# Linear attention in chunks of 64 tokens with a regrouped TensorE slot and a ring of six states

## The chip, the cores and the metric

The kernel runs on one core of a Trainium2 chip. The metric is the device time of one execution in microseconds (us). Three timed runs of the kernel before gave a median of 864.46 us (862.91 to 868.9). A profile was taken of one execution.

## The reference, cut to what matters

One transformer layer over 4 sequences of 2048 tokens of width 256: a causal linear attention with 16 heads of 16, then a mixture of 8 experts of which each token takes two. Around both stand layer norms whose scale, shift and gate come from a small product. The attention is written as a running state:

```
def step(carry, inp):
    S, z = carry
    q_t, k_t, v_t = inp                      # q, k = elu(.) + 1
    S = S + k_t[..., :, None] * v_t[..., None, :]
    z = z + k_t
    num = jnp.einsum('bhde,bhd->bhe', S, q_t)
    den = jnp.maximum(jnp.sum(z * q_t, axis=-1, keepdims=True), EPS)
    return ((S, z), num / den)
...
x = x + ga * attention(layernorm(x) * (1 + ca) + sa)
x = x + gb * moe(layernorm(x) * (1 + cb) + sb)   # top 2 of 8, capacity 1280 rows each
```

## The kernel before, in words

The tokens are 64 tiles of 128, in 16 groups of four. The first phase, up to about 600 us, is attention and routing; the second reads the rows gathered for each expert and adds their results to the output.

The first phase is one list of slots, `run_slots`, which every engine walks with its own `slot_`. Slot n carries the attention of tile n, a quarter of the projections of group n // 4 + 1 (stage 1), a quarter of the second layer norm and row building of group n // 4 - 1, and a quarter of the routing of group n // 4 - 2. The four slots of a group are told apart by q = n % 4. The order within a slot is written out by hand on each engine, and each engine runs it strictly in that order; semaphores hold it until another engine's result is there.

For a tile, the 128 tokens stand against each other in one block. TensorE makes the scores k.q of two heads at a time (`scores`, L1340, 256 columns, 32 rows deep, into the four banks of `SCW`). VectorE multiplies them by the triangle `tri` in two halves of 128x1024 (`masked_scores`, L967). Into the same banks (`OB`) TensorE then adds two things: the queries times the state carried from all earlier tiles (`from_state`, L1360) and the masked scores times the values (`from_tile`, L1376, in two halves of eight heads). Each value row has 17 columns, so that the 17th gives the denominator. The keys are transposed (`key_rows`, L1366), copied by ScalarE to `Kn` (L820) and multiplied by the values to update the state in PSUM (`add_to_state`, L1391, bank `SB`); VectorE copies it to `Sbd` (`state`, L992). The sums leave through ScalarE (`OTs`, L839). One slot later they are transposed to rows (`head_rows`, L1350, bank `MD`), normalised by VectorE (`normalise_heads`, L976 to L983), transposed back (`attention_columns`, L1401, bank `MA`), copied (`ATs`, L824) and multiplied by the output weights (`out_product`, L1409, again bank `MD`). VectorE adds the result to x (`add_out`, L1114).

Stage 1 goes through the banks `PJ[0]` and `PJ[1]`: the transposes of the normalised rows (L1420, slot 0), the four query and key blocks (`stage1_qk`, L1436, two each in slots 1 and 2; ScalarE reads each twice, as EX and as QT or KT, L676 and L677, and VectorE finishes it in `phi`, L1001), and the two value blocks (`stage1_v`, L1446, slot 3). The transposed rows are scaled to `hT_raw` (L658), rounded to a high part (L665) and GpSimd makes the low part (L544). Routing shares the banks: `h2_transposes` (L1468, slot 0), the copies `h2T` (L801), `logits` (L1488), `logit_rows` (L1495, slot 1), `take` (L754), and `positions` (L1555 to L1559, slot 3). GpSimd scatters the rows to the experts' buffers, eight scatters a group (L494), each released by a step of TensorE.

TensorE's order in a slot of the kernel before is: scores; routing rows; first stage 1 block; positions; head rows of tile n - 1; from-state; (stage 1 transposes in slot 0); key rows; first half from-tile; attention columns; second half from-tile; state update; out product of tile n - 1; second stage 1 block; logits in slot 0.

## Time and profile before

| | us |
|---|---|
| median of three timed runs | 864.46 |
| span of the profiled execution | 864.3 |
| TensorE busy in it (PE) | 812.9 |
| VectorE (DVE) | 577.1 |
| ScalarE (ACT) | 488.9 |
| GpSimd (POOL) | 478.9 |

The page gives each engine's busy time and costliest groups of instructions. PE is TensorE's matmuls and PEld its weight loads, which overlap them. L1376 is line 1376 of the kernel. In the timeline a number in brackets is the time that the engine stood idle before the row, and the arrow names what released it.

### The profile page before, as it was taken

To read this page: it belongs to the slowest core of one execution; us is meant where nothing else is said; L and a number is where in the kernel's file an instruction comes from. 1 tells how busy PE (TensorE), PEld (TensorE's weight loads), DVE (VectorE), ACT (ScalarE), POOL (GpSimd) and SP (SyncE) were. 2 spreads that over 40 slices of the span, in tenths; PEclk is the share of its full clock that TensorE was granted. 3 is DMA by queue.
4 is the path that set the end of the run, shared out by engine and by line. 5 is a ranking of instruction groups with operands and counts; after the bars stand their busy time and mean duration, and the time that the engine had idled before them with its cause. 6 is when DMAs were issued, how large, how long until landed. Compare 5 with 4: busy or idle time off the path is not lost.

```text
span 864.3 us, 24637 instructions
## 1 busy us (share of the span) xinstructions
PE 812.9 (94%) x9527; PEld 667.7 (77%) x9527; DVE 577.1 (67%) x1740; ACT 488.9 (57%) x1003; POOL 478.9 (55%) x621
## 2 busy tenths in 40 slices
PE   6899999999999999999999999868999998999994
PEld 4677776777767767777777677558999998999994
DVE  5676676777777867868767767750756655767762
ACT  4665666656757656657657565442655453555551
POOL 2203345664664665646656646564556657666654
PEclk9999999999999999999999999988999999999997
DMA  5589903333332233322222212334476666676653
GB/s 195 186 247 282 284 26 114 85 87 110 67 120 89 76 114 87 86 101 70 72 71 62 64 50 41 62 85 148 82 158 120 151 145 122 152 152 158 121 100 37
DMA packets 71426, 99.02 MB, mean 115 GB/s; under 512 B 7810, under 2 KB 52866, under 8 KB 71320
## 3 DMA queue, kind: packets, MB, share of 16 engines
q1 hardware_dynamic: 38744, 53.93, 23.0%
q0 software_dynamic: 21760, 31.66, 16.2%
q10 hardware_dynamic: 10816, 11.96, 4.5%
q8 instruction: 72, 1.18, 0.6%
q14 instruction: 34, 0.28, 0.1%
HBM read 46.84 MB, written 63.36 MB: 127 GB/s over the span
## 4 chain that ended last, share of the span: by engine, by line
PE 75%; POOL 6%; DMA 6%; DVE 4%; issue 4%; ACT 3%; POOLq 0%; another core or an unknown queue 0%; SPq 0%; DVEq 0%; ACTq 0%
PE PJ L1436 10%; PE SCW L1662 9%; PE MD L1409 7%; PE SCW L1340 7%; PE SCW L1376 7%; PE PJ L1446 5%; PE SCW L1677 4%; PE SCW L1360 4%; PE SCW L1401 4%; DMA out<-EX,desti 3%; PE MD L1350 3%; PE SCW L1366 2%; PE SB L1677 2%; PE MD L1677 2%; POOL hT L544 2%
## 5 line engine op out<-in xcount | busy, mean ns | idle before, releaser
L494 POOL DMA_INDIRECT slot_rows<-Hrow,sloti x128 | 128.0, 1000 | 129.6 <-PE SCW L1366 48.5
L967 DVE TENSOR_TENSOR Sm<-SCW,tri 128x1024 f32<-128x1024 f32 x128 | 150.7, 1219 | 70.9 <-PE SCW L1340 69.0
L612 POOL DMA_INDIRECT out<-EX,desti x80 | 125.3, 1566 | 24.1 <-POOL idle L440 11.4
L1436 PE MATMUL PJ<-hT,w_qkv 128*128 128x512 f32 x384 | 110.1, 419 | 2.4 <-POOL hT L544 1.9
L440 POOL TENSOR_TENSOR idle<-mhalf 128x1 f32<-128x1 f32 x136 | 58.9, 433 | 78.5 <-DVE EX L1270 47.2
L1436 PEld LDWEIGHTS PJ<-hT,w_qkv 128*128 128x128 f32 x384 | 69.7, 190 | 25.1 <-issue 6.5
L1376 PE MATMUL SCW<-Sm,VA 128*17 128x128 f32 x2048 | 80.8, 275 | 0.2 <-issue 0.2
L1409 PE MATMUL MD<-w_og,ATs 128*128 128x256 f32 x256 | 73.2, 404 | 4.7 <-ACT ATs L824 2.8
L676 ACT ACTIVATE EX<-PJ 128x512 f32<-128x512 f32 x64 | 37.9, 592 | 67.5 <-PE PJ L1436 67.5
L1340 PE MATMUL SCW<-QM,KT 32*128 32x256 f32 x1024 | 73.3, 400 | 0.6 <-ACT OTs L839 0.5
L680 ACT ACTIVATE N<-X,nb,rs 128x256 f32<-128x256 f32 x128 | 66.4, 591 | 12.3 <-POOL nb L554 12.2
L872 ACT ACTIVATE VA<-SCW 128x512 f32<-128x512 f32 x80 | 47.8, 598 | 39.3 <-PE SCW L1662 37.8
L544 POOL TENSOR_TENSOR hT<-N,hT 128x512 fp32r<-128x512 f32 x30 | 37.7, 1278 | 54.3 <-ACT hT L665 54.3
L552 POOL TENSOR_TENSOR rs<-vp,mhalf 128x4 f32<-128x4 f32 x31 | 31.7, 1024 | 60.8 <-DVE vp L1008 59.4
L1677 PE MATMUL SCW<-w_qkv,QS 128*128 128x256 f32 x416 | 61.8, 285 | 3.1 <-DVE QS L1242 3.1
L1662 PE MATMUL SCW<-KS,w_g 128*128 128x256 f32 x480 | 61.9, 285 | 0.4 <-DVE KS L1234 0.4
L1376 PEld LDWEIGHTS SCW<-Sm,VA 128*17 128x17 f32 x2048 | 44.9, 96 | 21.8 <-issue 21.8
L1662 PE MATMUL SCW<-VS,w_g 128*128 128x256 f32 x480 | 61.8, 285 | 0.0
L1340 PEld LDWEIGHTS SCW<-QM,KT 32*128 32x128 f32 x1024 | 46.4, 184 | 18.9 <-issue 15.5
L1677 PEld LDWEIGHTS SCW<-w_qkv,QS 128*128 128x128 f32 x416 | 56.4, 192 | 3.3 <-issue 3.3
L1662 PEld LDWEIGHTS SCW<-KS,w_g 128*128 128x128 f32 x480 | 58.2, 189 | 0.7 <-DVE KS L1234 0.7
L764 ACT ACTIVATE QM<-QT,parity 128x256 f32<-128x256 f32 x128 | 57.8, 505 | 0.8 <-DVE KT L1001 0.8
(215 smaller groups left out, 1825.4 us busy)
## 6 DMA issues: line engine op xcount, KB each, us to landing
Hrow<-slot_rows SPq DMA_DIRECT2D x32, 516.0 KB
slot_rows<-erow ACTq DMA_DIRECT2D x1, 10400.0 KB, 46.7
X<-x SPq DMA_DIRECT2D x16, 512.0 KB, 4.8
out<-X SPq DMA_DIRECT2D x16, 512.0 KB
Hrow<-mod_rows SPq DMA_DIRECT2D x16, 512.0 KB
QT<-slot_rows SPq DMA_DIRECT2D x8, 516.0 KB
slot_rows<-Hrow,sloti POOLq DMA_INDIRECT x128
N<-wd SPq DMA_DIRECT2D x4, 512.0 KB
```

The costliest lines, as they stand in the source:

```text
L440: pool.tensor_tensor(idle[:, k:k + 1], mhalf[:, 0:1], mhalf[:, 0:1], ALU.add).then_inc(breath, 1)
L494: pool.indirect_dma_start(xe, bass.IndirectOffsetOnAxis(sloti[:, par, k, t:t + 1], 0), Hrow[:, par, t, :], None, bounds_check=last_slot, o ...
L612: pool.indirect_dma_start(out, bass.IndirectOffsetOnAxis(desti[s % 2][:, a:a + 1], 0), Ys[s % 2][:, a, :], None, bounds_check=TOK - 1, oob ...
L680: act.activation(dst, X[:, bass.ds(xt, 1), :].rearrange("p a d -> p (a d)"), ACT.Identity, scale=rs[:, t:t + 1], bias=nb[:, t:t + 1]).then ...
L764: act.activation(QM[:, 1 - tp, odd], QT[:, g1, :, q1 * P:(q1 + 1) * P], ACT.Copy, scale=parity[:, odd:odd + 1]).then_inc(q_masked, 1)
L967: dve.tensor_tensor(o.rearrange("p c (k w) -> p c k w", k=2), SCW[:, 2 * pair:2 * pair + 2, :].rearrange("p k (c w) -> p c k w", c=DC), tr ...
L1340: last = mm(SCW[:, r, cc * 2 * P:(cc + 1) * 2 * P], KT[rows, gp, cc, q * P:(q + 1) * P], QM[rows, tp, :, cc, :], start=True, stop=True)
L1376: last = mm(OB[32 * a:32 * a + SW, part, cc, :], VA[:, gp, q, h, :], Sm[:, tp, h, :], start=False, stop=(part == 1), skip_group_check=True)
L1409: last = mm(MD[:, 0:D], ATs[:, cc, :], w_og[:, cc, :], start=(cc == 0), stop=(cc == DC - 1))
L1436: last = mm(PJ[m % 2][:], w_qkv[:, wp, cc, m * P:(m + 1) * P], hT[:, hp, cc, :], start=(cc + i == 0), stop=(cc == DC - 1 and i == len(SPLI ...
L1662: last = mm(SC[hh][:, (f % 2) * BW:(f % 2 + 1) * BW], w_g[:, wp, cc, f * P:(f + 1) * P], XT[par][:, xp, cc, :], start=(cc + i == 0), stop= ...
L1677: last = mm(((MA, KR), (MD, SB))[par][a][:, 0:D], hid[par][hp][:, f, a * P:(a + 1) * P], WD[k][wp][:, f, :], start=(f + i == 0), stop=(f = ...
```

## The change

A tile is treated as two chunks of 64 tokens. `part(k)` is chunk k's half of the partitions, `CH` is 64.

- Scores are made only within a chunk: 16 products of 64 x 128 columns (32 instructions) in place of 8 of 128 x 256. The mask is one operation of 128x1024 with the small triangle `tri64`.
- `from_tile` is one block of 32 products, 64 rows deep and 64 columns wide. `from_state` has 16 products of 64 columns, each chunk with its own state.
- The state is no longer summed in PSUM. `add_to_state` makes each chunk's own product in one of the two banks of `PM`, which are also `PJ[1]` and `MD`. VectorE multiplies both by the head mask into `Snew` and adds them one after the other into a ring `Sbd` of six states. It does so for tile n + 1 in slot n. In slots 0 to 2 of a group this product stands ahead of from-state and from-tile, in slot 3 behind them.
- The transposes of the keys of tile n + 1 and of the attention rows of tile n - 1 are one block (`columns_and_keys`), and ScalarE copies both at once into `AK`.
- `head_rows` moves to the same tile's slot, behind the out product, whose output moves from `MD` to `SB`. `positions` moves to `SB` for most groups.
- The second layer norm's deviations and normalising copies move from slot 2 to slot 1; on ScalarE the transposed copies of stage 1 and their high parts stand together behind `OTs`; what releases GpSimd's scatters is renamed to the new steps.

```diff
+            def scores(T):
+                q, gp = T % 4, (T // 4) % 2
+                ...
+                pe.wait_ge(q_masked, 2 * T + 2)
+                at_least(pe, ot_done, T)
+                for cc in range(DC):
+                    for k in range(2):
+                        for r in range(4):
+                            rows = slice(32 * r, 32 * r + 32)
+                            last = mm(SCW[part(k), r, cc * P:(cc + 1) * P],
+                                      KT[rows, gp, cc, q * P + CH * k:q * P + CH * k + CH],
+                                      QM[rows, T % 2, :, cc, part(k)], start=True, stop=True, skip_group_check=True)
+                last.then_inc(sc_full, 1)
+            def columns_and_keys(n):
+                at_least(pe, state_read, n + 1 if tile_ok(n) else n)
+                if tile_ok(n - 1):
+                    pe.wait_ge(an_done, n)
+                    ...
+                        last = pe.transpose(MD[:, cc * P:(cc + 1) * P], a[:, cc * P:(cc + 1) * P], ident[:])
+                if tile_ok(n + 1):
+                    t = n + 1
+                    pe.wait_ge(phi_done, 4 * (t // 4) + 4)
+                    at_least(pe, ak_done, n + 1)
+                    ...
+                last.then_inc(ak_full, 1)
+            def from_tile(T):
+                ...
+                for cc in range(DC):
+                    for b in range(2):
+                        for k in range(2):
+                            for a in range(4):
+                                r, s = 2 * b + a // 2, a % 2
+                                last = mm(OB[32 * a:32 * a + SW, k, b, cc, :], VA[part(k), gp, q, head(cc, r, s), :],
+                                          Smh(T % 2)[part(k), r, 2 * cc + s, :], start=False, stop=True,
+                                          skip_group_check=True)
+                last.then_inc(av_done, 1)
+            def add_to_state(n, g, routed, step):
+                t = n + 1
+                q, gp = t % 4, (t // 4) % 2
+                pe.wait_ge(ak_done, n + 2)
+                ...
+                        if n % 4 == 1:
+                            pe.wait_ge(h_raw, 2 * N + 2)
+                        else:
+                            pe.wait_ge(pj_read, 6 * N + 2 * (n % 4) - 2)
+                    if routed and step == "columns":
+                        pe.wait_ge(h2t_done, 2 * g + 2)
+                    if routed and step in ("first", "pick"):
+                        pe.wait_ge(taken, g + 1)
+                ...
+                for cc in range(DC):
+                    for k in range(2):
+                        for r in range(4):
+                            h = head(cc, r, 0)
+                            last = mm(PM[32 * r:32 * r + 32, k, cc * 2 * SW:(cc + 1) * 2 * SW],
+                                      Kn[part(k), cc * P + 32 * r:cc * P + 32 * r + 32],
+                                      VA[part(k), gp, q, h:h + 2, :].rearrange("p s w -> p (s w)"),
+                                      start=True, stop=True, skip_group_check=True)
+                last.then_inc(state_full, 1)
```

VectorE's state and ScalarE's new copy:

```diff
+            def state(n, first, second):
+                t = n + 1
+                dve.wait_ge(state_full, t + 1)
+                ...
+                dve.tensor_tensor(Snew[:], PM[:, :, 0:DC * 2 * SW].rearrange("p k (h w) -> p k h w", h=DC * 2),
+                                  headmask[:].unsqueeze(1).to_broadcast([P, 2, DC * 2, SW]), ALU.mult
+                                  ).then_inc(state_read, 1)
+                first()
+                dve.wait_ge(state_read, t + 1)
+                dve.tensor_tensor(state_at(2 * t + 1), state_at(2 * t), Snew[:, 0], ALU.add).then_inc(sbd_half, 1)
+                second()
+                dve.wait_ge(sbd_half, t + 1)
+                ...
+                    dve.tensor_tensor(state_at(2 * t + 2), state_at(2 * t + 1), Snew[:, 1], ALU.add).then_inc(sbd_done, 1)
+            def columns_and_keys(n):
+                c0, c1 = (0 if tile_ok(n - 1) else D), (2 * D if tile_ok(n + 1) else D)
+                act.wait_ge(ak_full, n + 2)
+                ...
+                act.activation(AK[:, c0:c1], MD[:, c0:c1], ACT.Copy).then_inc(ak_done, 1)
```

TensorE's slot after the change, and ScalarE's part that stands between TensorE's waits:

```diff
                 if tile_ok(n) and n > 0:
-                    scores(T, q, gp, tp)
-                if routed and step in ("first", "pick"):
-                    logit_rows(g)
+                    scores(n)
+                if n >= -1 and q != 3:
+                    columns_and_keys(n)
 ...
+                if n >= -1 and q == 3:
+                    columns_and_keys(n)
+                if routed and step in ("first", "pick"):
+                    logit_rows(g)
                 if routed and step == "place":
                     positions(g, gn)
 ...
+                if n >= -1 and tile_ok(n + 1) and q != 3:
+                    add_to_state(n, g, routed, step)
+                if tile_ok(n):
+                    from_state(n)
+                    from_tile(n)
+                if n >= -1 and tile_ok(n + 1) and q == 3:
+                    add_to_state(n, g, routed, step)
 ...
                 if stage1 and q == 0:
                     stage1_transposes(G, gn)
+                if tile_ok(n - 1):
+                    out_product(n - 1)
                 if tile_ok(n):
-                    key_rows(T, q, gp)
-                    from_tile(T, G, q, gp, tp, 0)
 ...
+                    head_rows(n)
```

```diff
# ScalarE
+                if n >= -1 and q == 3:
+                    columns_and_keys(n)
+                if routed and step in ("first", "pick"):
+                    take(lg, lg_ps[:, :, 0:E], lg_full, g)
 ...
                 if stage1 and q == 0:
-                    stage1_hi(G, 0)
-                    stage1_hi(G, 1)
-                if group_ok(gn - 1) and q == (2 if gn < GROUPS - 1 else 1):
-                    ln2_norm(it, G, gn, gp)
+                    for cidx in range(DC):
+                        stage1_transposed(G, cidx)
+                        stage1_hi(G, cidx)
+                if tile_ok(n) and tile_ok(n + 1) and q != 0:
+                    next_tile_queries(n)
+                if group_ok(gn - 1) and q == 1:
+                    ln2_norm(G, gn)
```

## Rows read from the trace of the kernel before

**Rows 1.** Busy time by stretches: the stretch, its length, each engine's busy us.
```profile
core 0: us, PE busy (x) PEld busy (x) DVE busy (x) ACT busy (x) POOL busy (x), PEclk, DMA share, GB/s
95.00:503.00 408.00, 399.37 (x5465) 296.14 (x5462) 302.90 (x961) 262.48 (x588) 238.97 (x332) 1.00 0.29 88
```

**Rows 2.** TensorE's timeline, line 1420 in slot 0: start us, us, engine, line.
```profile
29.61 0.66 PE L1420 MATMUL PJ<-ident,N 128*128 128x128 f32 x4
...
95.00 1.09 PE L1420 MATMUL PJ<-ident,N 128*128 128x128 f32 x8
...
502.87 1.09 PE L1420 MATMUL PJ<-ident,N 128*128 128x128 f32 x8
```

**Rows 3.** The chain that ended last, in order of time: start us, us, what.
```profile
302.68 0.37 PE SB L1386 x2
303.04 0.26 PE SB L1391 x16
...
304.94 1.07 PE SCW L1340 x16
...
307.66 0.44 PE MD L1350 x4
308.10 0.59 PE SCW L1360 x16
308.69 0.37 PE SCW L1366 x2
309.06 0.56 PE SCW L1376 x16
...
324.21 1.62 PE PJ L1446 x12
```

**Rows 4.** TensorE's timeline, waits within a routed group.
```profile
320.03 0.37 PE L1391 MATMUL SB<-VA,Kn 128*32 128x34 f32 x13 [0.51 <-issue]
320.61 1.13 PE L1409 MATMUL MD<-w_og,ATs 128*128 128x256 f32 x4 [0.21 <-ACT ATs L824]
```

**Rows 5.** ScalarE's timeline in the same group.
```profile
301.00 0.78 ACT L658 ACTIVATE N<-PJ,saca 128x512 f32<-128x512 f32 x1 [1.41 <-PE PJ L1420]
...
303.57 1.16 ACT L665 ACTIVATE hT<-N 128x512 fp32r<-128x512 f32 x2
...
306.31 0.20 ACT L754 ACTIVATE lg<-PJ 128x32 f32<-128x32 f32 x1 [0.24 <-PE PJ L1495]
307.70 0.60 ACT L676 ACTIVATE EX<-PJ 128x512 f32<-128x512 f32 x1 [1.19 <-PE PJ L1436]
308.19 0.59 ACT L677 ACTIVATE QT<-PJ 128x512 f32<-128x512 f32 x1
309.10 0.38 ACT L820 ACTIVATE Kn<-SCW 128x256 f32<-128x256 f32 x1 [0.32 <-PE SCW L1366]
...
321.51 2.08 ACT L680 ACTIVATE N<-X,nb,rs 128x256 f32<-128x256 f32 x4 [0.47 <-POOL nb L554]
```

**Rows 6.** VectorE's timeline in the same group.
```profile
303.38 0.23 DVE L992 SCALAR_TENSOR_TENSOR Sbd<-SB,headmask 128x68 f32<-128x68 f32 x1 [1.10 <-PE SB L1391]
...
306.08 2.35 DVE L967 TENSOR_TENSOR Sm<-SCW,tri 128x1024 f32<-128x1024 f32 x2 [0.92 <-PE SCW L1340]
...
327.43 1.25 DVE L1001 SCALAR_TENSOR_TENSOR KT<-KT,EX 128x512 f32<-128x512 f32 x1
```

**Rows 7.** A scatter of GpSimd and the ScalarE copy that waited beside it, timelines.
```profile
318.47 1.27 POOL L494 DMA_INDIRECT slot_rows<-Hrow,sloti  x1 [0.30 <-issue]
320.17 0.38 ACT L824 ACTIVATE ATs<-SCW 128x256 f32<-128x256 f32 x1 [1.79 <-PE SCW L1401]
```

**Rows 8.** TensorE's timeline in the last tiles: waits for the mask.
```profile
543.06 0.67 PE L1360 MATMUL SCW<-QT,Sbd 32*64 32x128 f32 x16 [0.30 <-DVE Sm L967]
...
559.47 0.67 PE L1360 MATMUL SCW<-QT,Sbd 32*64 32x128 f32 x16 [1.67 <-DVE Sm L967]
```

More of the change, by code:

```diff
@@ L311, in group_ok, with head, part @@
             return 0 <= n < GROUPS
-        def halves(it, back):
-            return (it - back) // 2 if isinstance(it, int) else (it - back) // 2
-        def headslot(r):
-            return [2 * r, 2 * r + 1]
+        def head(cc, r, s):
+            return cc * HC + 2 * r + s
+        def part(k):
+            return slice(CH * k, CH * k + CH)
         @block.sync
@@ L1173, in slot_ @@
                 if tile_ok(n):
-                    masked_scores(T, 0, tp, n)
-                    masked_scores(T, 1, tp, n)
-                if routed and step == "place":
-                    if tile_ok(n - 1):
-                        normalise_heads(T, between, lambda: None)
-                elif tile_ok(n - 1):
-                    normalise_heads(T, between, between)
-                while n == TILES - 2 and small[0] < 9 or n == TILES - 1 and small[0] < 13:
-                    between()
-                if q == 0 and group_ok(gn + 2) and gn >= 1:
-                    ln1_stats(it, G, gp)
+                    masked_scores(T)
                 if stage1 and q >= 2:
@@ L1397, in attention_columns, with out_product @@
-            def attention_columns(T):
-                pe.wait_ge(an_done, T)
-                a = An[:].rearrange("p h e -> p (h e)")
-                for cc in range(DC):
-                    last = pe.transpose(MA[:, cc * P:(cc + 1) * P], a[:, cc * P:(cc + 1) * P], ident[:])
-                last.then_inc(at_full, 1)
-            def out_product(T, n):
-                if n % TPB == 1:
-                    pe.wait_ge(w_og_done, n // TPB + 1)
-                pe.wait_ge(at_done, T)
-                for cc in range(DC):
-                    last = mm(MD[:, 0:D], ATs[:, cc, :], w_og[:, cc, :], start=(cc == 0), stop=(cc == DC - 1))
+            def out_product(T):
+                if T % TPB == 0:
+                    pe.wait_ge(w_og_done, T // TPB + 1)
+                pe.wait_ge(ak_done, T + 3)
+                at_least(pe, x1_done, T)
+                g, step = routing(T + 1)
+                if group_ok(g) and step == "place" and g < GROUPS - 2:
+                    pe.wait_ge(route, NR * g + 15)
+                for cc in range(DC):
+                    last = mm(SB[:, 0:D], ATs[:, cc, :], w_og[:, cc, :], start=(cc == 0), stop=(cc == DC - 1))
@@ L1574, in slot_ @@
                 if tile_ok(n) and n > 0:
[L1575 to L1577 removed]
+                    scores(n)
+                if n >= -1 and q != 3:
+                    columns_and_keys(n)
                 if n == TILES - 3:
```

408 lines of the change are left out of this document (182 added, 226 removed).

## The prediction

> **What bounds the kernel now.** I read the busy time by stretches first [rows 1]. From 95 to 503 us, where attention and routing run together, TensorE is busy for 399.4 of 408.0 us, VectorE for 302.9, ScalarE for 262.5 and GpSimd for 239.0, at a granted clock of 1.00 (the 2.4 GHz level). The experts, which follow it, are untouched by the diff. So TensorE's stream of work sets the pace of the part that changes. The starts of the transposes of line 1420 count it out [rows 2]: they come once a group of four tiles. From 95.00 to 502.87 there are 12 groups, so 33.99 us a group; from 29.61 to 95.00 there are two, 32.7 each. The chain in order of time stays on TensorE from block to block [rows 3], with few waits in it: about 0.7 us a group, of the kind in [rows 4].
>
> **How TensorE's blocks are priced.** An fp32 product shows as two instructions, so eight products are x16. Four whole-array transposes take 0.44 us, so 128 columns cost 0.11 us an instruction. The from-tile block, 128 columns in tiles 17 columns wide, has 16 instructions in 0.56 us: four sets of four, with 4 x 0.11 = 0.44 for the sets and 0.12 for the change of tile shape behind them. Four tiles pass in the time of one. The scores: 1.07 us = 4 sets x 0.22 (256 columns) + 0.19. From-state: 0.59 = 4 x 0.11 + 0.15. The state update (34 columns): 0.26 = 4 x 0.035 + 0.12, so an instruction of a set takes no more than 0.009 us to issue [rows 3]. What no row shows is a set of eight tiles, two row tiles by four column tiles, or four by two, which the change makes of its scores, from-tile and state products.
>
> **The change, part by part, on TensorE, for one tile.** I take a set of eight as the larger of its columns' time and 8 x 0.009 = 0.07 us; its bounds are 0.055 (64 columns alone) and, if only four pass at once, twice the set of four.
> Scores: 32 instructions of 128 columns are 4 sets of 8: 4 x 0.11 + 0.19 = 0.63, against 1.07, so -0.44 (bound: 8 x 0.11 + 0.19 = 1.07, no gain).
> From-tile: 64 instructions of 64 columns, 8 sets: 8 x 0.06 + 0.12 = 0.60, against 2 x 0.56, so -0.52 (bounds 0.56 and 16 x 0.055 + 0.12 = 1.00).
> From-state: the same four tiles at half the columns, 8 x 0.055 + 0.15 = 0.59, no change.
> State update: 32 instructions, 4 sets x 0.065 + 0.1 = 0.36, +0.10. The identity product that brings the state back (L1386, 0.37 once in eight tiles) goes, -0.05.
> Transposes of keys and of the attention rows become one block of four, 0.50 against 0.37 + 0.37, and lose one change of shape: -0.24, but the change of shape before the state update costs +0.1. Head rows stand next to other whole-array work: -0.09. The out product loses the overlap with the projection behind it: +0.1.
> Sum: -0.44 - 0.52 + 0.10 - 0.05 - 0.24 + 0.10 - 0.09 + 0.10 = -1.04 a tile, -4.2 a group. The 0.7 us of waits now seen goes with it, since the out product then uses columns copied at the slot's start: -4.9.
>
> A row speaks for cheap narrow instructions: 16 of the state update, 34 columns each, pass in 0.26 us, 0.016 each with the change of shape included [rows 3]. The Trainium skill speaks against them: "TensorEngine Tiling (Array Packing)", Performance Considerations, says that each matmul carries an overhead of about 60 cycles and that no tiling should be drawn from a dimension that is already small; "TensorE: Matmul & The Clock Gate", Part 1, has a floor of about 25 ns from start to start. By that floor the from-tile block would take 1.6 us in place of my 0.60; the trace disagrees where it can be read.
>
> **The other engines.** VectorE masks 128x1024 values a tile once instead of twice; two take 2.35 us [rows 6], so -1.15. The state becomes a product and two additions in place of one operation of 0.23 [rows 6]: about +0.5. Per group VectorE falls by 2.6 us. ScalarE copies once 512 columns in place of twice 256 (0.38 each [rows 5]): -0.17. None becomes the bound. The four normalising copies of the second layer norm (2.08 [rows 5]) move from slot 2 to slot 1, ahead of the copies of the second query block, whose bank the state update of slot 2 needs; that update comes 2.7 us after the block ends (0.63 + 0.5 + 1.6), and ScalarE is through about 2.1 after it: no wait, but close. The ring of six states lets VectorE write ahead of what from-state still reads, so it adds no wait. GpSimd's scatters keep their number, 8 a group; only what releases them changes.
>
> **What the new order takes back.** The state products now lie in the two banks of PM, which are also PJ[1] and MD. So the state update must wait for whatever still reads there, and in slots 0 to 2 from-state, from-tile, the out product and the scatters that these release stand behind it. Reading ScalarE's durations and the order of the code, for a routed group:
> (a) Slot 1: the state update waits for `taken`. ScalarE, after the projection ends, does EX, QT (starts 0.49 apart) and then lg (0.20) [rows 5]: 0.2 + 0.5 + 0.5 + 0.2 + 0.15 back to TensorE, less 0.09 for the row transpose: 1.45 us.
> (b) Slot 0: it waits for both copies h2T. The merged copy comes ahead of them: the eight transposes end 0.9 after the key block, the copies at 0.2 + 3 x 0.5 + 0.1, and 0.15 back: 1.0 us.
> (c) Slot 0: the logits wait for both h_raw. Copy 0, its high part and copy 1 (0.78, 0.53, 0.78 [rows 5]) now follow the transposes in one run, 2.4 us with the ways, covered by out product and head rows (1.35): 1.05 us. Before, three more blocks lay between.
> (d) Slot 3: the key transposes wait for phi of K. Mask 1.2, then phi up to 1.25 [rows 6], with 0.15 between each, against the value block's 1.6 [rows 3] and the attention rows' 0.3: 0.8 us.
> (e) Slot 0: the attention rows of the tile before wait for VectorE, which in slot 3 also carries nine placing steps: 0.5 us.
> (f) Head rows wait for the copy of the same tile's sums, 0.2 + 0.6 + 0.15 after from-tile, against an out product of 0.94: nothing, or 0.1.
> Together 4.8 us. A routed group comes to 34.0 - 4.9 + 4.8, about 33.8: -0.2. There are 13 of them: -2.6.
>
> The first two groups have no routing: (a), (b) and (c) are absent. There the key copy (0.9 us, with nothing of the slot to cover it), the mask, h_lo and (d) leave about 2 us of waits against 4.2 saved, and waits now there shrink: -3 each, -6. In the last four tiles, without projections, TensorE waits for the mask itself, 0.3 to 1.67 us a time [rows 8]; with a mask 1.15 shorter and a serial chain of a slot otherwise the same I take 1 us a tile: -4. Before tile 0 its keys must be transposed, copied and multiplied: +1.
> Sum: 864.3 + 1 - 6 - 2.6 - 4 = 852.7; the profiled execution's 864.3 is within 0.2 of the median, so I give 852 us.
>
> **The rivals.**
> Shorter waits, 834 us. (a) to (e) are sums along one path; where the slot before ends late for another reason they overlap. If 1.4 us a group goes, 13 x 1.4 = 18: 834. For it: VectorE and ScalarE have over 100 us idle in [rows 1]. Against it: (a) to (c) start from TensorE's own block of the slot, so nothing early helps. Chance 0.17.
> Scatters in the way, 864 us. Around a scatter TensorE's signals come late: ScalarE idles 1.79 us ahead of ATs, and TensorE stands still for 0.51, near the 1.27 us scatter at 318.47 [rows 4, 7]. The new order has more hand-overs in a slot; 0.9 us more a group gives 13 x 0.9 = 12, which eats the gain. Chance 0.16.
> Eight tiles do not pass together, slower: 904 us. Scores gain nothing (+0.44 on my sum), from-tile takes 1.00 (+0.40), the state update 8 x 0.035 + 0.1 (+0.02): 0.86 x 64 = 55, less some wait that it covers: +52. It decides from 0.19 us a tile on (12 / 64). For it: no row has more than four tiles in a set. Against it: sets of four rows and sets of four columns both pass whole. A half of it, 878 us, stands for a set of eight that is merely slower. Together 0.18.
> A fixed price for each instruction, slower: 967 us. If half the columns do not shorten an instruction, its price lies between the state update's 0.016 us and from-tile's 0.56 / 16 = 0.035 [rows 3]; the middle, 0.025, times the 160 packed instructions that replace 80 in a tile is 4.0 us, against 0.63 + 0.59 + 0.60 + 0.36 = 2.2 in my sum, so 1.8 x 64 = 115. Against it: the 0.016. Chance 0.03. The floor of the Trainium skill's page "TensorE: Matmul & The Clock Gate" lies there.
>
> **How the numbers follow.** My forecast, 840 to 864 with 852 in its middle, has 0.46. A measurement of this kernel tells about 1% from no change: 855.8 to 873.1 is "same". Of my own case 0.33 lies under 855.8 and 0.13 above it; with the 0.17 of shorter waits, faster is 0.50; same is 0.13 + 0.16 = 0.29; slower 0.21. The range is 834 to 880: it leaves out the full case of four at a time, the fixed price and the far end of the shorter waits.
>
> **What the profile of after would show.** From-tile x64 in about 0.6 us and scores x32 in about 0.63, or else twice that. TensorE idle before the state update in slot 1 (about 1.4) and slot 0 (about 1), before the logits (about 1) and before the key transposes of slot 3 (0.8), released by ScalarE and VectorE. Groups of 33.8 us when routed, near 29.7 before that. I am wrong if these waits are absent, or if sets of eight take over 0.09 us.

## The result: 8.4% slower, and the profile after

| us | before | after |
|---|---|---|
| median | 865.19 (4 runs) | 937.54 (4 runs) |
| ratio, 95% interval | | 1.0844 [1.0791, 1.0897] |
| span of the profiled execution | 864.3 | 934.8 |
| first start of the stage 1 transposes [rows 2] | 29.6 | 36.1 |
| from there to the last start, 14 groups | 473.3 | 532.6 |
| behind it | 361.4 | 366.1 |

Some executions of a kernel are over 1.5% slower than its fastest, and the ratios leave them out: of experiment 5's ten they are five (872 to 879 us; with all ten its ratio would be 1.01), of experiment 9's four one (1734 us).

The forecast was 852, the range 834 to 880; the time lies far outside it. Nearly all of the loss, 59.3 of 70.5 us, is in the stretch that the argument was about.

Busy time by stretches of the kernel after: stretch, length, busy us of each engine, granted clock, DMA share, GB/s. The first row answers to [rows 1].

```profile
95.00:503.00 408.00, 337.88 (x8278) 272.19 (x8277) 249.40 (x880) 230.22 (x479) 205.46 (x283) 0.93 0.28 86
...
200.00:300.00 100.00, 86.34 (x2116) 69.91 (x2117) 66.17 (x235) 57.28 (x121) 55.89 (x79) 0.94 0.26 87
300.00:400.00 100.00, 82.53 (x2123) 66.46 (x2122) 64.90 (x226) 59.23 (x124) 55.35 (x74) 0.98 0.26 90
400.00:500.00 100.00, 83.41 (x1992) 67.33 (x1990) 59.15 (x215) 56.00 (x115) 53.75 (x75) 0.90 0.28 69
```

TensorE was busy for 399.4 of 408 us and is now busy for 337.9, but no other engine is busier either: VectorE fell from 302.9 to 249.4, ScalarE from 262.5 to 230.2. Nobody became the bound. TensorE stands still, and its granted clock is 0.90 to 0.98 where it was 1.00, so part of the time at its 1.2 GHz level.

The chain that ended last, kernel after, in order of time (start us, us, what; L1343 scores, L1374 from-state, L1389 from-tile, L1422 state update, L1446 out product):

```profile
294.62 0.36 PE SCW L1343 x4
294.99 2.10 issue
297.08 1.03 PE SCW L1343 x28
...
307.28 0.62 PE SCW L1343 x32
307.90 0.37 PE PM L1355 x2
308.27 0.22 PE PM L1361 x2
...
311.01 0.10 ACT lg L764
311.11 0.14 issue
311.25 0.36 PE PM L1422 x22
311.61 0.62 PE SCW L1374 x32
312.23 0.76 PE SCW L1389 x64
...
320.21 0.37 PE SCW L1374 x10
320.58 0.43 issue
321.01 0.62 PE SCW L1374 x20
...
329.84 0.26 PE PM L1422 x19
330.10 5.16 issue
```

Two things are to be seen. The blocks cost nearly what was forecast: scores x32 0.62 (forecast 0.63), from-state 0.62 (0.59), keys and attention rows 0.37 + 0.22 (0.50), from-tile 0.76 (0.60). Eight tiles do pass together. And TensorE stops where it has nothing to wait for: after 4 of the 32 instructions of the scores for 2.10 us, after 10 of from-state for 0.43, after the state update for 5.16. The code has no wait inside a block, so no semaphore explains a stop behind the fourth instruction. "issue" means that the profile shows nothing that was waited for. Between the first and the last start of L1459 there are 13 "issue" stops of over 1.6 us, 36.1 us in all; [rows 4] shows the longest kind of before, 0.51.

The short stop is of another kind than the long ones. It comes at the same place in nearly every group, and it begins 1.0 us after a scatter of GpSimd has begun:

```profile
319.56 1.14 POOL L507 DMA_INDIRECT slot_rows<-Hrow,sloti  x1 [0.30 <-issue]
...
321.01 0.62 PE L1374 MATMUL SCW<-QT,Sbd 32*64 32x64 f32 x22 [0.43 <-issue]
```

The 0.51 us of [rows 4] begins 1.05 us after the scatter at 318.47 of [rows 7]. In the 14 groups there are 12 such stops, 5.4 us, after the change and 6, 2.9 us, before it. They stay in experiment 1, and the profiles of experiments 4 to 6 and 8 to 12, which ran on other chips, have next to none.

TensorE's waits over the whole span (line waited for, releaser, us in total, times, longest), kernel after:

```profile
PE PM L1422 <- ACT lg L764: 16.2, 13, 1.2
PE SCW L1389 <- issue: 15.7, 15, 2.7
PE SB L1446 <- issue: 14.8, 4, 5.2
PE PM L1422 <- ACT h2T L814: 12.4, 14, 1.4
PE SCW L1343 <- issue: 11.2, 5, 3.0
PE PM L1528 <- issue: 8.1, 9, 0.9
```

The rows with ScalarE as releaser are the predicted waits (a) and (b), L1528 is (c). The "issue" rows of L1389, L1446 and L1343 were in no step.

The 5.16 us stop beside the transfers around it. First two timeline rows (SPq issues a DMA), then the DMA queues' packets in 326 to 333 us and in 333 to 334 us:

```profile
325.66 0.39 SPq L367 DMA_DIRECT2D Hrow<-mod_rows  x1
...
335.26 1.86 PE L1446 MATMUL SB<-w_og,AK 128*128 128x256 f32 x4 [5.16 <-issue]
```
```profile
q1 hardware_dynamic: 511, 0.51, 26.7%
...
q8 instruction: 1, 0.02, 6.0%
q1 hardware_dynamic: 17, 0.01, 4.1%
```

Once a group SyncE spreads the sequence's row of gates over `Hrow`, 512 KB (L367). Its packets run from 327.0 to 333.2. In all that time the queue of kind "instruction" moves nothing; its one packet starts at 333.06, as the load ends, and TensorE goes on 2.2 us later. At 294.78 a fetch starts, again as q1 falls silent, and TensorE goes on at 297.08. It is so for all 13 long stops: TensorE goes on 2.20 to 2.54 us after the start of a packet of this queue. The same queue over the whole execution, kernel before and kernel after (packets, MB, share):

```profile
q8 instruction: 72, 1.18, 0.6%
```
```profile
q8 instruction: 113, 1.85, 0.8%
```

A packet is 16 KB and takes about 1 us. From this came theory F: **instruction supply**. TensorE's instructions come from memory in these packets, over the DMA engines that carry the bulk transfers. The change doubles the packed instructions (160 a tile for 80), so that what TensorE holds no longer lasts through a bulk transfer. Its rivals: sets of eight that are slow or stall by themselves; the new order and its hand-overs; the scatters.

### The profile page after: what moved, and what is told of

It is laid out like the page before. It is cut to its first block, busy times and chain, and to the rows that moved or that the text cites. A ratio compares the mean times of both kernels' runs of the same rounds, so it can differ in the third digit from the quotient of the medians.

```text
span 934.8 us, 35097 instructions
## 1 busy us (share of the span) xinstructions
PE 790.6 (85%) x14631; PEld 680.3 (73%) x14631; DVE 556.4 (60%) x1805; ACT 485.1 (52%) x941; POOL 479.9 (51%) x621
## 4 chain that ended last, share of the span: by engine, by line
PE 73%; issue 10%; DVE 7%; ACT 3%; POOL 2%; DMA 2%; DVEq 0%; POOLq 0%; ACTq 0%; SPq 0%
PE SCW L1703 12%; PE SB L1446 8%; PE SCW L1718 6%; PE SCW L1389 6%; PE PM L1475 5%; PE SCW L1374 5%; PE PJ L1475 5%; PE SCW L1343 4%; PE PM L1718 3%; PE PM L1434 3%; PE SB L1718 3%; PE PM L1422 2%; DVE Sm L975 2%; PE PM L1355 2%; PE PM L1361 2%
## 5 line engine op out<-in xcount | busy, mean ns | idle before, releaser
L975 DVE TENSOR_TENSOR Sm<-SCW,tri 128x1024 f32<-128x1024 f32 x64 | 78.1, 1221 | 43.0 <-PE SCW L1343 37.3
L453 POOL TENSOR_TENSOR idle<-mhalf 128x1 f32<-128x1 f32 x136 | 61.5, 452 | 75.3 <-DVE EX L1273 45.8
L1446 PE MATMUL SB<-w_og,AK 128*128 128x256 f32 x256 | 81.4, 444 | 16.3 <-issue 14.8
L1134 DVE TENSOR_TENSOR X<-X,SB 128x256 f32<-128x256 f32 x64 | 26.8, 419 | 113.1 <-PE SB L1446 113.1
L839 ACT ACTIVATE OTs<-SCW 128x512 f32<-128x512 f32 x64 | 38.3, 598 | 106.4 <-PE SCW L1389 106.4
L1389 PE MATMUL SCW<-Sm,VA 64*17 64x64 f32 x4096 | 59.0, 226 | 15.8 <-issue 15.7
L1446 PEld LDWEIGHTS SB<-w_og,AK 128*128 128x128 f32 x256 | 48.8, 212 | 22.3 <-issue 12.0
L782 ACT ACTIVATE AK<-PM 128x512 f32<-128x512 f32 (+1 forms) x66 | 38.5, 583 | 49.1 <-PE PM L1361 47.4
L1389 PEld LDWEIGHTS SCW<-Sm,VA 64*17 64x17 f32 x4096 | 44.3, 95 | 23.2 <-issue 18.7
L565 POOL TENSOR_TENSOR rs<-vp,mhalf 128x4 f32<-128x4 f32 x31 | 32.5, 1047 | 52.9 <-DVE vp L1030 52.6
L1343 PE MATMUL SCW<-QM,KT 32*64 32x128 f32 x2048 | 48.0, 288 | 13.5 <-issue 11.2
L1703 PEld LDWEIGHTS SCW<-VS,w_g 128*128 128x128 f32 x480 | 58.3, 189 | 0.0
```

Source lines behind the costliest of these rows:

```text
L453: pool.tensor_tensor(idle[:, k:k + 1], mhalf[:, 0:1], mhalf[:, 0:1], ALU.add).then_inc(breath, 1)
L975: dve.tensor_tensor(Smh(T % 2), SCW[:, :, 0:2 * P].rearrange("p r (m i) -> p r m i", i=CH), tri64[:].unsqueeze(1).unsqueeze(1).to_broadcas ...
L1343: last = mm(SCW[part(k), r, cc * P:(cc + 1) * P], KT[rows, gp, cc, q * P + CH * k:q * P + CH * k + CH], QM[rows, T % 2, :, cc, part(k)], s ...
L1389: last = mm(OB[32 * a:32 * a + SW, k, b, cc, :], VA[part(k), gp, q, head(cc, r, s), :], Smh(T % 2)[part(k), r, 2 * cc + s, :], start=False ...
L1446: last = mm(SB[:, 0:D], ATs[:, cc, :], w_og[:, cc, :], start=(cc == 0), stop=(cc == DC - 1))
L1703: last = mm(SC[hh][:, (f % 2) * BW:(f % 2 + 1) * BW], w_g[:, wp, cc, f * P:(f + 1) * P], XT[par][:, xp, cc, :], start=(cc + i == 0), stop= ...
```

## The experiments

Ratios are to the kernel before on the same chip, with the 95% interval; chips differ, so times of different calls are not compared.

**1. The changed kernel without the later gate loads.**

```diff
-                at_least(sp, sent[k], i * 128)
-                sp.dma_start(Hrow[:, k, :, D + 4:ROW], mod_rows[...]).then_inc(gb_in[k], 16)
+                if isinstance(i, int):      # groups 0 and 1 only
+                    sp.dma_start(Hrow[:, k, :, D + 4:ROW], mod_rows[...]).then_inc(gb_in[k], 16)
```

> The changed kernel, without the load of the gate row into Hrow for groups 2 to 15 (the first two groups keep it), so the gates of the later batches are left out; nothing else differs. Theory F (instruction supply): the change raises TensorE's matmuls from 9527 to 14631, and its instruction fetches land only when the 6.5 us gate load that shares the DMA engines with them has ended; TensorE then stands still for 2 to 5 us with nothing to wait for. Without the loads most of the long stalls ahead of TensorE go: the groups of 37 to 43 us fall to 33.5 to 35, the time to 885 to 905. Rival C (clock and hand-overs: the stalls are the slot's own waits, and the clock falls by them): the load only touches GpSimd's rows, so the time stays within 5 us of 937.

Measured: 903.01 us, 1.0461 [1.0409, 1.0513], inside F's span. The stretches:

```profile
200.00:300.00 100.00, 85.77 (x2233) 69.44 (x2235) 70.53 (x247) 62.83 (x132) 58.84 (x84) 1.00 0.23 82
300.00:400.00 100.00, 87.03 (x2287) 70.73 (x2280) 70.21 (x250) 63.38 (x132) 59.83 (x83) 1.00 0.21 78
400.00:500.00 100.00, 86.45 (x2268) 70.12 (x2266) 69.47 (x243) 62.49 (x133) 58.86 (x83) 1.00 0.16 56
```

Only four stops over 1.6 us are left, all before 164 us (13.2 us), and the clock is 1.00 again. The ten groups from 188.8 us on take 33.5 to 35.7 us, 34.2 in the mean, where the forecast had 33.8. The loads cost this kernel 3.8 points. Most of what is left over the forecast lies in the groups before 188.8 us and outside of the 14.

**2. The kernel before without the same loads.**

> The kernel before without the gate loads of groups 2 to 15. Theory F: its fetches are also late, but the instructions already held last over the load, so nothing or up to 6 us is gained: 858 to 865. If the gate load cost time in another way (GpSimd, memory), before would gain as the changed kernel does, over 15 us.

Measured: 866.74 us, 0.9992 [0.9957, 1.0027]. The kernel before loses nothing to the same transfers. It takes both, the load and the longer program.

**3. The kernel before with each packed product cut in two by columns.** Nothing of the change is in it but the number of instructions: 160 a tile, the same order, waits, bytes and tiles (sets of four).

```diff
-                    for r in range(4):
+                    for o, r in [(o, r) for o in range(2) for r in range(4)]:
-                        last = mm(SCW[:, r, cc * 2 * P:(cc + 1) * 2 * P], KT[...], QM[rows, tp, :, cc, :], ...)
+                        last = mm(SCW[:, r, (cc * 2 + o) * P:(cc * 2 + o + 1) * P], KT[...], QM[rows, tp, o, cc, :], ...)
```

(likewise from-state, from-tile and the state update)

> The kernel before, with scores, from-state, from-tile and state update cut in two by columns: 160 instructions a tile in place of 80 for the same columns, the same four tiles at once, the same banks, waits and order. Theory F: as many instructions as the changed kernel has, so the same long stalls without a cause that the profile names, at the end of the gate loads: 900 to 935 us. Rival C, or any theory in which the new order or the sets of eight are to blame: only a few ns an instruction, 865 to 880 us.

Measured: 940.8 us, 1.0895 [1.0837, 1.0953]: a loss as large as the changed kernel's, with none of its order, its sets of eight or its waits, and over the 900 to 935 that I expected. The instruction queue and the chain of this kernel (L1398 is the state update):

```profile
q8 instruction: 112, 1.84, 0.8%
```
```profile
289.61 0.57 PE SCW L1381 x32
290.18 0.06 PE SB L1398 x8
290.24 3.21 issue
293.45 0.38 PE SB L1398 x23
```

The cut adds 64 x 80 x 2 = 10,240 instructions (each product is two), and the queue 112 - 72 = 40 packets: 256 instructions a packet, exactly. Seven stops of over 1.6 us add up to 20.6 us, each ending 2.26 to 2.46 us after the start of a packet. The sets of eight and the new order fall with this run as causes of the long stops: it has neither.

That the loss has the size of the changed kernel's is in part luck, since it is made up otherwise. The 14 groups are 61.5 us longer than before. Of these 20.6 are the long stops; 11 are short stops 0.9 to 1.2 us after the start of a scatter (44 of them, 14.0 us, against 6 and 2.9 before); about 13 are what the cut instructions themselves cost more (0.23 us a tile, experiment 4); and the granted clock, at 0.50 for 24 us of this stretch, can stand for up to 12 more, which leaves some 5 open. So the scatters have a share here, though not in the long stops.

The page "Runtime: NRT & Kernel Launch" of the Trainium skill, section on instruction fetch mechanics, says that an engine's instructions come by a DMA queue of its own in blocks of 16 KiB, 256 instructions; the 40 packets agree. It also gives TensorE room for 2048 instructions and calls the cost of a block mostly hidden; an estimate from that room is that it could go on for 50 us at the 41 instructions a us of this kernel (8416 + 8414 in 408 us). Here it stops beside a transfer of 6.5 us, so the measurement decides against both statements for this kernel.

**4. The same cut without the gate loads.**

> The kernel before with its instructions cut in two (as in b_split) and without the gate loads of groups 2 to 15. Theory F: the stalls at the end of gate loads go, as they did in the changed kernel (34 us), so 900 to 915, and groups of 35 to 36.5 us stay. If the extra instructions cost by themselves alone, the time stays at 935 to 945.

Measured: 882.85 us, 1.0335 [1.0282, 1.0388]. That is less than I expected, also on the scale of the first chip (1.0335 x 865 = 894). Without the loads the groups from the third on take 33.6 to 35.3 us. Of the cut's 9.0%, 5.6% is gone; but this chip's profile has none of the short stops behind scatters, which made 1.3% in experiment 3, so about 4.3% is what comes through the loads. The other 3.4% is what the early stretch and the instructions themselves cost: in the stretch of [rows 1] the cut scores, from-state, from-tile and state update are busy for 56.3 + 33.2 + 60.6 + 23.4 us in 47 tiles, 3.69 a tile, against 55.0 + 32.4 + 60.8 + 17.8 in 48, 3.46: 0.23 x 64 = 15 us, 1.7%. The rest lies before 110 us, where three stops are left (8.5 us): the first two groups take 80.5 us, against 65.4 before, 1.8%.

**5. The kernel before with only scores and from-state cut: 112 instructions a tile.**

> The kernel before with only the scores and from-state cut in two by columns: 112 packed instructions a tile in place of 80, against 160 in the full split (which took 1.0895 of the time of before). Same order, waits, bytes and work of the other engines. Theory F (TensorE stands still once the instructions that it holds run out before the next fetch arrives): the reserve still covers most of a 6.5 us gate load, so few or no stalls over 1.6 us after the early fill: ratio 1.00 to 1.02. Rival (each added instruction costs the same, 75 us for 80 a tile): 32 of 80, ratio 1.036 (1.03 to 1.04). Second rival (order or set size of the change is what costs, not the number): ratio 0.998 to 1.002.

Measured: 1.0012 [0.9963, 1.006]. Page and stretch:

```profile
q8 instruction: 88, 1.44, 0.7%
```
```profile
95.00:503.00 408.00, 401.87 (x6992) 314.38 (x6990) 299.48 (x958) 263.03 (x588) 238.60 (x332) 1.00 0.32 89
```

Again the packets follow the count: 16 more for 64 x 32 x 2 = 4,096. A price for each added instruction would have given 1.036 (1.030 without the short stops of experiment 3). So the loss doesn't grow with the count in proportion: a loss that is clear of the noise sets in between 112 and 160 a tile. A gate load with the 2.2 us behind it lasts 8.7 us; in that time TensorE passes 233 instructions before, at the rate of [rows 1] (5465 + 5462 in 408 us), 298 here (6992 + 6990), and 389 in the kernel of experiment 1 (2233 + 2235 in 100 us). Two of these rates pass without a stop over 1.6 us, the third doesn't.

The trace of the changed kernel shows that what TensorE holds when the load begins isn't one number: it hangs on how long ago the last fetch started. Of the 12 gate loads from 180 to 600 us, six began 3.7 to 4.5 us after a fetch; after 282 to 369 more instructions of TensorE, counted in the trace with the weight loads, it stood still, all six times. The other six began 0.2 to 1.8 us after a fetch, and 397 to 415 instructions passed without such a stop. In the kernel of this experiment 227 to 342 passed in a load, once 342 with the last fetch 4.8 us before it, without such a stop: the limit is no sharp number.

**6. The changed kernel with half of from-tile** (first eight heads; 128 packed instructions a tile).

```diff
-                for cc in range(DC):
+                for cc in range(1):
```

> The changed kernel with from_tile for the first eight heads only: 32 of a tile's 160 packed instructions are left out, and half the sums within the chunk with them. On TensorE that is 0.38 us a tile, 64 x 0.38 = 24 us, if nothing but its work counts: 913. Theory F: it also takes a fifth off the instruction stream, so most of the long stalls go as well: 870 to 895.

Measured: 863.84 us, 1.0112 [1.0069, 1.0156]; 97 packets, and 12.8 us of "issue" stops over 1.6 us in place of 36.1. The work left out is 64 x 0.38 = 24 us, 2.8% of before; the ratio falls by 7.3 points. So here what a row charges for the instructions was the smaller part of their price. This run mixes the two effects and doesn't separate them as experiment 3 does.

**7. The changed kernel, `logit_rows` behind the scores and `take` right behind `lgT`.** It takes away wait (a).

```diff
+                if routed and step in ("first", "pick"):
+                    logit_rows(g)            # TensorE: behind scores(n), was behind the key columns
...
+                    take(lg, lg_ps[:, :, 0:E], lg_full, g)   # ScalarE: behind lgT, was behind QT
```

> The changed kernel with the row transpose of the logits ahead of the key block and its copy (take) ahead of the merged copy, so that the state update of slot 1 no longer waits for it. The prediction's term (a) puts 1.45 us a group on this wait, 13 groups: 18 us less if it is on the path, 915 to 922. Theory F alone: the wait also gives the fetches time, so a part comes back as stalls: 920 to 932.

Measured: 925.15 us, 1.0671 [1.0613, 1.0728]. `lg` is through at 307.95 in the slot where it was needed at 311.1, and the 16.2 us of waits for L764 are gone; the kernel gains 1.7 points. Wait (a) was real and is a fifth of the loss.

**8. The same, with the gate loaded only where the sequence changes, in four pieces** (a complete computation; SyncE's loop over the groups is written out for it).

```diff
-                at_least(sp, sent[k], i * 128)
-                sp.dma_start(Hrow[:, k, :, D + 4:ROW], ...)
+                if i % 2 == 0:
+                    for t in range(GT):
+                        if i > 0: sp.wait_ge(x1_done, g * GT + GT + 2 + t)
+                        sp.dma_start(Hrow[:, k, t, D + 4:ROW], ...)      # 128 KB each
```

> The changed kernel, nothing left out: take ahead of the projection as in a_take, and the gate row loaded only where the sequence changes (8 loads in place of 16), each in four pieces that wait for a tile each. Theory F: nearly the gain of a_nogate (34 us) and that of a_take (12 us) together: 885 to 900. If only the whole absence of the load helps, 905 to 925.

Measured: 873.07 us, 1.0257 [1.0202, 1.0312]. Undisturbed groups take 31.4 to 32.5 us, below the 34.0 of [rows 2], also if the 12 us by which the kernel before is shorter on this chip are all taken from its groups (0.9 each); the two groups from 69 to 151 us take 41.6 and 40.2. So the change's saving on TensorE is there once the supply holds. What is left in its waits:

```profile
PE PM L1425 <- ACT h2T L819: 12.3, 14, 0.9
PE PM L1531 <- issue: 11.6, 13, 0.9
PE SCW L1392 <- issue: 8.6, 8, 1.8
PE SB L1449 <- issue: 8.2, 4, 5.8
```

**9. And one order in all slots: from-state, state update, from-tile.** It gives wait (b) the cover of from-state. In the same run ScalarE makes both transposed copies of stage 1 ahead of both high parts, so that the logits (wait (c)) wait for one operation less.

```diff
-                if n >= -1 and tile_ok(n + 1) and q != 3:
-                    add_to_state(n, g, routed, step)
                 if tile_ok(n):
                     from_state(n)
-                    from_tile(n)
-                if n >= -1 and tile_ok(n + 1) and q == 3:
+                if n >= -1 and tile_ok(n + 1):
                     add_to_state(n, g, routed, step)
+                if tile_ok(n):
+                    from_tile(n)
 ...                                          # ScalarE
                     for cidx in range(DC):
                         stage1_transposed(G, cidx)
+                    for cidx in range(DC):
                         stage1_hi(G, cidx)
```

> The changed kernel with take first, gates loaded only where the sequence changes (in tile-sized pieces), and one order of the three state blocks in all slots: from-state, then the state product of the next tile, then from-tile. The state product now has from-state (0.62 us) ahead of it in slots 0 to 2, so the waits for ScalarE ahead of it (0.88 in slot 0, 1.25 less what take gave back in slot 1) should shrink to 0.3 or less, and from-tile and what follows move up. Instruction supply (theory F) still stands: the same 160 packed instructions a tile, so the early groups of 40 us beside the 10.4 MB fill stay. Expected: later groups 31 to 32.5 us, total 8 to 18 us under the kernel with only the first two edits; ratio 1.005 to 1.017. Rival (the remaining time is all supply, waits only hide it): total unchanged, ratio 1.02 to 1.03.

Measured: 872.47 us, 1.0165 [1.0088, 1.0242]. In its waits from 200 to 500 us `h2T` is left with 0.3 us (7.9 in experiment 8), and the logits are down to

```profile
PE PM L1532 <- issue: 2.0, 7, 0.3
...
PE SCW L1393 <- issue: 10.1, 6, 2.3
```

but from-tile's stops grew to 10.1 us (3.7 in the same stretch of experiment 8). The two waits went as expected; the ratio is at the far end of the 1.005 to 1.017 that I expected, and its interval reaches into that of experiment 8, so a gain isn't shown. A faster TensorE seems to run into its supply more often; nine stops of over 1.6 us add up to 23.8 us, against five with 14.7.

**10. And the 10.4 MB fill of the experts' rows in 20 pieces, over slots 4 to 10.**

> As a_new1, and the 10.4 MB fill of the experts' rows is cut into 20 transfers, issued three a slot in slots 4 to 10 in place of one transfer near the start. Theory F: TensorE's instruction fetches no longer stand behind a long queue of one fill; the two early groups of 40 to 42 us come down towards 34 to 36, 8 to 16 us less in all; ratio 0.985 to 1.0. Rival (the early groups are long because of something else than the fill's queue, or the pieces fill the same DMA engines as densely): no change beside a_new1.

Measured: 864.22 us, 1.0121 [1.0083, 1.0158], not told apart from experiment 9, and not the 0.985 to 1.0 that I expected. The pieces moved the stops, they did not remove them (timeline, TensorE):

```profile
90.79 0.62 PE L1408 MATMUL SCW<-Sm,VA 64*17 64x64 f32 x39 [3.30 <-issue]
...
123.37 1.65 PE L1465 MATMUL SB<-w_og,AK 128*128 128x256 f32 x3 [7.18 <-issue]
```

Between 111 and 123 us pieces of the fill and the four pieces of a gate load, issued at 110.55, are in the engines together, and the longest stop of all lies there, 7.18 us; a fetch starts at 121.10. That more spacing would remove it was not tried.

**11 and 12. The kernel before, with attention columns and out product of tile n - 1 later in the slot.** From the analysis of before: its own 0.7 us a group of waits ([rows 4]) come from the out product's standing too close behind the columns. Columns go behind the state update, the out product behind the second stage 1 block; in slots 1 to 3 first.

```diff
+                late_cols = stage1 and q > 0          # 12: q in (1, 2)
-                if tile_ok(n - 1):
+                if tile_ok(n - 1) and not late_cols:
                     attention_columns(T)
 ...                                                   # and again, if late_cols, behind add_to_state
```

> The kernel before with as many instructions, and the attention columns of slots 1 to 3 behind the state update, next to the second projection block, the out product behind that. It saves two changes of tile shape (0.11 each) and the wait for ATs, some 0.3 us in 45 slots: 848 to 858. If the order of the copies on ScalarE costs as much, no change.

Measured: 851.65 us, 0.9984 [0.9948, 1.0019]. The waits for `ATs` went and another came:

```profile
PE PJ L1468 <- ACT VA L772: 11.8, 13, 0.9
```

The second layer norm's transposes of slot 0 wait for `VA`, which ScalarE now copies later in slot 3. So slot 3 was left as it was:

> The kernel before, in which the attention columns and the out product of slots 1 and 2 alone stand later in the slot (columns behind the state update, out product behind the second projection block). In slot 3 they stay where they were, since there the move made the transposes of the second layer norm wait 0.9 us for VA's copy. No added instruction. Order theory: the short waits of TensorE for ATs (0.2 to 0.5 us each) go and nothing new comes: 0.4 to 0.8 us a group, 5 to 10 us, ratio 0.988 to 0.995. Rival (the waits were covered elsewhere or come back at another place): ratio 0.998 to 1.002.

Measured: 840.57 us, 0.9859 [0.9793, 0.9924]: the one version here that is faster than both kernels. All groups from 29.5 us on take 32.1 to 32.7 us, and idle times over 0.15 us between the first and last start of L1420 add up to 4.4 us (9.5 before):

```profile
95.00:503.00 408.00, 406.23 (x5736) 309.14 (x5735) 317.35 (x997) 270.09 (x612) 252.74 (x341) 1.00 0.31 91
```

It gained more than its waits: 12.6 us on the same chip, 0.9 a group, of which the waits make 5.1 / 14 = 0.4. The chain shows another part: where nothing stands between the halves of from-tile they pass as one block of 32, 1.00 us in place of 0.56 twice, so a change of tile shape is gone as well, 0.12 in each of two slots. That makes 0.6; the remaining third is open. It may be more: 2.9 of the 9.5 us of before are the short stops behind scatters, which the profiles of this chip don't show in any kernel.

## Why the prediction was wrong, point by point

The sum of the forecast against the trace, 14 groups of four tiles: 36.1 us of stops that it had not; 14 x 1.9 = 27 us of slower work at a granted clock of 0.93; 9 us because from-tile takes 0.76; and about 6 us less of short waits. With its own -8.4 for this stretch that makes +58, against the measured +59.3. The 1.9 is worked out thus: idle times over 0.15 us add up to 91.4 us, so the work took (532.6 - 91.4) / 14 = 31.5 us a group; before it was (473.3 - 9.5) / 14 = 33.1, less 4.2 forecast, plus 0.6 for from-tile, is 29.6. Experiment 1, at a clock of 0.98, bears it out: there the work of a group took 29.9.

**The step that failed** is the pricing of TensorE's blocks: "an instruction of a set takes no more than 0.009 us to issue", and with it the silent assumption that 80 more instructions a tile, 160 of them with the weight loads, cost nothing but their columns. The row was read rightly and the blocks confirm it. But it prices instructions that are at hand. That they must be brought stood in no step, though the page of before has the row: 72 packets in the queue "instruction", 1.18 MB, in the same engines as 99 MB of data. The number of packets to come could have been worked out (19,054 instructions of TensorE before, 29,262 after), and how full the engines are at each gate load is in the windows. What could not be read from before is how much TensorE holds. In the trace its place is taken by the 36.1 us of stops and the 27 us of slower work that went with them.

**The other mechanisms.** (a) 1.45 forecast, 1.25 seen, every routed group. (b) 1.0: 0.78 to 0.88, once 1.36. (c) 1.05: 0.94. (d) 0.8: 0.13 to 0.67, and 0.15 in most groups. (e) 0.5: 0.37 to 0.48, in six groups. (f) nothing, and no wait for that copy is seen. Idle times apart from the long stops add up to 55.3 us in the 14 groups, against 12 x 4.8 + 2 x 2 = 62 forecast; but 5.4 of them are the short stops behind scatters and 7.0 shorter stops that end 2.0 to 2.7 us after a packet's start, so what was forecast measures about 43. Three of the changed kernel's routed groups, free of long stops, take 33.4 to 33.6 us: the forecast was 33.8. (Its own sum, 34.0 - 4.9 + 4.8, gives 33.9, so -1.3 and not -2.6 for 13 groups, which doesn't matter here.) The step-by-step reading of the engines' orders found the waits that came and priced (d) much too high; the mis-sized term among the blocks is from-tile (0.76 for 0.60), whose first 32 instructions start mostly about 7 ns apart and the later ones about 17 a pair.

**Ahead of tile 0** the forecast was +1, measured +6.5. The first scores wait 2.31 us for VectorE's copies out of `SCW` (L950 to L952), which its new order puts behind the first state's product and additions, and TensorE's own blocks there stand in series with ScalarE's copies (0.74 us for `AK`). I had counted only the work. **The last tiles**: -4 forecast; all that lies behind the last start is 4.7 us longer. The mask waits did shrink (0.58 where 1.67 was), but `positions` waits longer for VectorE's `masks` (2.10 and 1.41 us, 0.69 before), from-tile of the last tile comes in pieces of 5 or 6 instructions, and the granted clock from 611 to 666 us is 0.78 (0.88 before, 545 to 600).

**The rivals.** "Shorter waits" was not the issue. "Scatters in the way" saw a real thing, stops that begin 1.0 us after a scatter's start, but they grew by 2.5 us in the 14 groups and not by 12. "Eight tiles do not pass together" is refuted by the blocks. "A fixed price for each instruction" (967, chance 0.03) named the right variable, the number of instructions, and the wrong law: experiment 5 shows none of it up to 112 a tile. Its evidence against it, 0.016 us an instruction, stays true.

**The clock.** That it falls behind stops and not by the new blocks themselves is what experiment 1 shows: with the same blocks and no late stops it is 1.00 from 200 to 500 us. In the changed kernel's 14 groups the clock is at 0.50, the 1.2 GHz level, for 68 us in 12 stretches, and each of these begins during a stop of over 1.5 us or within 1.6 us behind it (for one, 0.50 from 297.4 to 300.6, behind the stop that ends at 297.08). I had taken a clock of 1.00 as given.

What stays open: how long TensorE's reserve is in full, why the fetch starts mostly at the end of a bulk transfer, why a scatter is followed by a short stop on some chips and not on others, and whether the changed kernel with its bulk transfers spread well enough would beat the kernel before; the best version of it that ran is 1.0121.

## What to carry to other kernels

Count instructions when products are cut smaller. A program's own instructions are a stream of data in the DMA engines, 256 to a packet; look at the queue of kind "instruction" in the page, work out what it becomes, and compare the instructions that the engine passes during the longest bulk transfer with what passed without a stop before. An "issue" stop in the middle of a block that has no wait points to this cause if a packet of that queue starts 2.2 to 2.5 us before its end; here a stop of 0.2 to 0.5 us that begins 1 us after a scatter was something else. Cutting the unchanged kernel's products in two, with nothing else moved, tests it; look then at what the loss is made of, and not at its size alone.

A wait that is removed shows its worth only when nothing else bounds the engine: two waits taken from the changed kernel (experiment 9) gave little, and a small reordering of a kernel with no such bound gave 1.4%.

## What the runs showed of the hardware that I had not expected

- TensorE resumes 2.2 to 2.5 us after a 16 KB packet of the queue "instruction" starts, though the packet itself takes about 1 us (333.06 to 335.26; 294.78 to 297.08; 121.10 to 123.37; so for all 13 long stops of the changed kernel).
- In the 12 gate loads of the changed kernel from 180 to 600 us that packet starts only in the last 0.1 to 1.1 us of the load, though the one from 327.0 to 333.2 takes only 26.7% of the engines' time. It is no fixed rule: in the kernel before one starts at 256.04, in the middle of the load from 253.5 to 260.1.
- Within a block without waits TensorE stands still for 0.2 to 0.5 us, beginning 1.0 us after a scatter of GpSimd begins (319.56 and 320.58), in the profiles of before, of after and of experiments 1 to 3 and 7, and next to never in those of three other chips.
- Stops cost more than their own time: in the stretches that hold them the granted clock is 0.90 to 0.98 where it was 1.00, 68 us of the 14 groups passed at the 1.2 GHz level, and by the estimate above 36.1 us of long stops went with 27 us of slower work.
- Sets of eight tiles (64 x 32) pass whole: 32 instructions of 128 columns in 0.62 us, where 16 of 256 columns in sets of four took 1.07 [rows 3].
